# A post-norm transformer layer with a codebook FFN: GpSimd's gathers written out, ScalarE's copies moved, the 64-row first tile packed

## What is computed

```python
# x: (2, 1024, 1024); 32 heads of 32
x = layernorm(x + attention(x, wq, wk, wv, wo))          # causal, rotary
Wg = codebook[idx_gate].reshape(2752, 1024)              # codebook: (16384, 8)
Wu = codebook[idx_up].reshape(2752, 1024)
Wd = codebook[idx_down].reshape(1024, 2752)
g = x @ Wg.T;  u = x @ Wu.T
y = (silu(g) * u) @ Wd.T
x = layernorm(x + y)
```

## Time and profile before

| | |
|---|---|
| median of 3 runs | 6821.02 us (6820.23 to 6821.85) |
| the profiled execution, own time | 6826.36 us |
| its span in the trace | 6824.5 us |
| TensorE busy | 98% of the span |
| VectorE, ScalarE, GpSimd busy | 68%, 55%, 72% |
| granted TensorE clock, mean | 0.996 |

### The profile page before, as it was taken

The page is one execution under the profiler, slowest core; times in us unless marked ns, Lnnn a source line. Parts: engine busy times, 40 slices in busy tenths (PEclk is TensorE's granted clock), DMA queues, the critical chain, the costliest instruction groups (busy, mean ns, idle before and its releaser), DMA issues.

```text
span 6824.5 us, 120862 instructions
## 1 busy us (share of the span) xinstructions
PE 6664.1 (98%) x29648; PEld 4072.6 (60%) x29648; DVE 4664.4 (68%) x11403; ACT 3779.4 (55%) x6691; POOL 4936.2 (72%) x5188
## 2 busy tenths in 40 slices
PE   9999899999999999999999999999999999999998
PEld 3444565666666566666666666666666666666664
DVE  3320788887777667777677776777667776677765
ACT  0000787886666555555555555555555555556553
POOL 7777777777777777777777777777777777777771
PEclk9999999999999999999999999999999999999999
DMA  4232222233333333333333333333333333233331
GB/s 138 65 87 49 53 59 54 53 84 72 82 80 76 66 72 66 74 73 73 74 70 72 75 73 71 68 74 73 74 68 73 75 72 74 66 74 72 74 68 64
DMA packets 480031, 491.50 MB, mean 72 GB/s; under 512 B 228672, under 2 KB 349248, under 8 KB 472896
## 3 DMA queue, kind: packets, MB, share of 16 engines
q10 hardware_dynamic: 298720, 425.47, 22.3%
q0 software_dynamic: 165888, 21.57, 7.8%
q1 hardware_dynamic: 14688, 36.48, 1.4%
HBM read 426.34 MB, written 56.72 MB: 71 GB/s over the span
## 4 chain that ended last, share of the span: by engine, by line
PE 75%; ACT 1%; issue 1%; DVE 0%; ACTq 0%; DMA 0%; DVEq 0%
PE ps L420 41%; PE ps L450 18%; PE ps L468 9%; PE ps L395 3%; PE ps L431 3%; PE ps L437 1%; ACT onehot L757 0%; ACT onehot L761 0%; PE ps L406 0%; PE ps L543 0%; DVE small L1045 0%; DVE onehot L996 0%; ACT arena L852 0%; DMA arena<-code_low 0%; DVE small L1048 0%
## 5 line engine op out<-in xcount | busy, mean ns | idle before, releaser
L209 POOL DMA_INDIRECT raw<-in_codebook_dram,idx_sb x5184 | 4936.0, 952 | 1758.1 <-DMA raw<-in_codebook_dram,idx_sb 1556.3
L996 DVE TENSOR_SCALAR_CACHE_REDUCE onehot<-arena,small 128x512 fp32r<-128x512 f32 x3845 | 2622.9, 742 | 1095.7 <-PE ps L420 1054.2
L420 PE MATMUL ps<-onehot,table 128*128 128x512 f32 x12288 | 3259.1, 416 | 28.2 <-ACT onehot L761 18.5
L420 PEld LDWEIGHTS ps<-onehot,table 128*128 128x128 f32 x12288 | 2289.5, 188 | 908.8 <-issue 380.5
L757 ACT ACTIVATE onehot<-arena,small 128x512 fp32r<-128x512 f32 x2307 | 1496.6, 713 | 1170.2 <-PE ps L420 1045.2
L761 ACT ACTIVATE onehot<-onehot,small 128x512 fp32r<-128x512 f32 x2307 | 1487.3, 708 | 0.0
L450 PE MATMUL ps<-big,arena 128*128 128x512 f32 (+1 forms) x2816 | 1297.0, 597 | 0.0
L450 PEld LDWEIGHTS ps<-big,arena 128*128 128x128 f32 (+1 forms) x2816 | 514.2, 187 | 595.0 <-issue 569.6
L1003 DVE SCALAR_TENSOR_TENSOR picked<-arena,small,ps 128x512 f32<-128x512 f16 x768 | 572.0, 745 | 161.9 <-PE ps L431 146.5
L468 PE MATMUL ps<-arena 128*128 128x512 f32 (+1 forms) x1408 | 652.7, 599 | 1.8 <-ACT arena L733 1.2
L908 DVE TENSOR_REDUCE small<-ps 128x1 f32<-128x384 f32 (+7 forms) x512 | 373.9, 751 | 297.8 <-PE ps L314 294.9
(11 more groups left out here) (72 smaller groups left out, 2719.5 us busy)
## 6 DMA issues: line engine op xcount, KB each, us to landing
arena<-code_low ACTq DMA_DIRECT2D x770, 256.0 KB
arena<-code_high ACTq DMA_DIRECT2D x770, 128.0 KB
raw<-in_codebook_dram,idx_sb POOLq DMA_INDIRECT x5184
gathered_units<-raw SPq DMA_DIRECT2D x39, 512.0 KB, 3.3
arena<-gathered_units ACTq DMA_DIRECT2D x19, 1024.0 KB
queries_keys<-arena ACTq DMA_DIRECT2D x16, 1024.0 KB, 4.0
arena<-queries_keys ACTq DMA_DIRECT2D x32, 512.0 KB
big<-queries_keys ACTq DMA_DIRECT2D x32, 512.0 KB
```

The source lines that it names most:

```text
L209: pool.indirect_dma_start(raw[:, s, n, :], None, codebook, bass.IndirectOffsetOnAxis(ap=idx_sb[:, s, n:n + 1], axis=0), engine_sem=describ ...
L420: last = mm(ps[:, 4 + s % 2, :], table[:, k, c, :], onehot[:, k, :], start=(k == 0 and c == 0), stop=(k == KLO - 1 and c == PIECES - 1))
L996: dve.tensor_scalar(onehot[:, k, :], lo_sb[:, s % 2, :], kp_sb[:, k:k + 1], None, ALU.is_equal, ALU.add, accum_out=hits[:, k:k + 1]).then_ ...
```

## The change

It has three parts. The two loops of GpSimd become straight-line code with constant waits. ScalarE's order in an attention round becomes e0, e1, copies 0 to 3, e2, e3, copies 4 and 5. In step 0, the 64 gate rows and the 64 up rows are laid side by side as one 128-column weight, so that one matmul makes both (gate in PSUM rows 0 to 63, up in rows 64 to 127): 32 matmuls instead of 64. SiLU writes its result to rows 64 to 127; VectorE multiplies twice, so that `hT` holds the same 64 rows twice, and `d_rep` is filled twice as well. The 32 down matmuls of step 0 then use rows 0 to 63 and 64 to 127 in turn. A slot of step 0 holds two FFN matmuls instead of three.

```diff
-                with pool.Fori(p0, p1) as p:
+                for p in range(p0, p1):
                     for s in range(2):
                         gather_unit(c, s, P, 16 * p + 16, 16 * p, 2 * P * p + (s * P - P + CS * CS))
...
-                one = mm(ps[0:ni, 2 * (t % 2) + m, :], w_rep[:, m, k, 0:ni], big1[:, k, t * N:(t + 1) * N],
+                one = mm(ps[:, 2 * (t % 2) + m, :], w_rep[:, m, k, :], big1[:, k, t * N:(t + 1) * N],
...
-                        pe.wait_ge(d_ready, 1 + step // NTILE)
+                        pe.wait_ge(d_ready, 2 + step // NTILE)
...
-                mm(ps[:, d % banks, :], d_rep[0:ni, h * P:(h + 1) * P], hT[0:ni, t * N:(t + 1) * N],
+                rows = half_rows(h % 2) if isinstance(step, int) and step == 0 else slice(0, P)
+                mm(ps[:, d % banks, :], d_rep[rows, h * P:(h + 1) * P], hT[rows, t * N:(t + 1) * N],
                    start=True, stop=True).then_inc(down_done, 1)
...
+                if isinstance(step, int):
+                    if n < CS * NT:
+                        gate_up(step, n // CS, 0, n % CS)
+                    else:
+                        down(step, n - CS * NT)
...
-                    for n in range(3 * s, 3 * s + 3):
-                        ffn_matmul(step, ni, n)
+                    beside = 2 if isinstance(step, int) else 3
+                    for n in range(beside * s, beside * s + beside):
+                        ffn_matmul(step, n)
...
                 if turned:
-                    copy_turned(i, u - 1, 0)
-                    copy_turned(i, u - 1, 1)
+                    for j in range(4):
+                        copy_turned(i, u - 1, j)
                 if scored:
                     exponent(i, u, 2)
-                if turned:
-                    copy_turned(i, u - 1, 2)
-                    copy_turned(i, u - 1, 3)
-                if scored:
                     exponent(i, u, 3)
...
-            def turned(count, ni, bank):
+            def turned(count, rows, bank):
                 act.wait_ge(turn_done, count)
-                act.copy(d_rep[0:ni, :].rearrange("p (h c) -> p h c", h=2),
-                         ps[0:ni, bank:bank + 2, :]).then_inc(d_ready, 1)
+                for out_rows in rows:
+                    act.copy(d_rep[out_rows, :].rearrange("p (h c) -> p h c", h=2),
+                             ps[0:out_rows.stop - out_rows.start, bank:bank + 2, :]).then_inc(d_ready, 1)
...
+                gates = (4, 8, 12, 16) if isinstance(step, int) and step == 0 else (2, 7, 13, 18)
...
-                                act.wait_ge(up_done, NT)
                                 act.wait_ge(taken, 3)
...
+                if isinstance(step, int) and step == 0:
+                    rows = half_rows(1)
+                    dve.tensor_tensor(hT[half_rows(0), cols], hT[rows, cols], ps[rows, 2 * (t % 2), :],
+                                      ALU.mult).then_inc(short_ready, 1)
+                    dve.wait_ge(short_ready, t + 1)
+                    dve.tensor_tensor(hT[rows, cols], hT[rows, cols], ps[rows, 2 * (t % 2), :],
+                                      ALU.mult).then_inc(hT_ready, 1)
+                else:
+                    dve.wait_ge(up_done, step * NT + (t + 1 - NT))
```

## The result

| | before | changed |
|---|---|---|
| median | 6821.14 us (5 runs, 6820.23 to 6822.56) | 6752.44 us (5 runs, 6748.72 to 6756.50) |
| ratio | | 0.9899, interval 0.9885 to 0.9913 |
| span of the profiled execution | 6824.5 us | 6750.5 us |
| step 0 | 222.6 us | 178.4 us |
| first to last of the 128 attention rounds | 869.2 us | 842.9 us |

The account below looks back on a forecast made before the run. TensorE's own work, three quarters of the span, bounds the kernel. Step 0's 44 plus the attention's 18 less 0.5 made 61.5 us, cut to 59.5 by GpSimd: 6821.0 - 59.5 = 6761.5 us, range 6753 to 6790.

Parts of the forecast that it names:

- the cap in the sum: At slot 20 of step 19, GpSimd's unit 38 cuts TensorE's gain from 61.5 to 59.5 us.
- GpSimd's room: Lead of unit 38 at slot 20 of step 19: 29.6 + 29 = 58.6 us, plus about 1 from ScalarE.
- The attention: ScalarE's new order saves TensorE's wait for copy 2 in rounds (1, 6): net 18 us less, bounds 5 and 24.
- The delay of 0.17: Attention rounds (0, 7) end later, delaying the next (1, 6) round: 0.17 us, taken off 0.75, times 32.
- Step 0, slots 0 to 15: Gate and up slots go from 6.57 to 5.36 us, plus 1 from later SiLU: 20.4 us less.
- Slots 16 to 31: Step 0's down slots go at VectorE's pace, 5.46 us each: 85.4 us against 110.3, 24 less.
- Step 0 together: Both halves of step 0: 20.4 + 24 = 44 us less, 34 if the matmul pairs don't overlap.
- The gathers don't get faster: Rival: the loop-turn gaps come back in straight-line code, holding TensorE at slot 20 of step 19; 6790 us, 1 in 10.
- slower: straight-line code is fetched too slowly: Rival: over 10,000 GpSimd instructions in a row slow each gather; at 0.02 us more, 6892 us; 3 in 100.
- The row halves don't overlap: Rival: step 0's down matmuls on different row halves run in turn; gain 51.5, time 6769 us, 1 in 10.
- ScalarE's order gives next to nothing: Rival: the new attention order gives only 5 us; gain 49 or less, time 6772 to 6778, 2 in 10.
- More than forecast: Rival: GpSimd's other pauses shrink too; gain 61.5, or up to 67 with 24 in the attention; 6754 to 6759, 1 in 10.

Follow-up runs that it names:

- e1_gathers_only: The kernel before with GpSimd's loops written out and nothing else: 6821.7 us, ratio 0.9998.
- e2_loops_kept: The changed kernel with GpSimd's two loops put back: 6785.3 us, ratio 0.9942 to the kernel before.
- e3: The kernel before with ScalarE's new order in the attention and nothing else: 6798.2 us, ratio 0.9963.
- e4: The kernel before with the packed step 0 only, GpSimd's loops and ScalarE's old order kept: 6786.0 us, ratio 0.9948.
- e7: The changed kernel with all 32 down matmuls of step 0 on rows 0 to 63: 6768.6 us, ratio 0.9918 to the kernel before.
- e8: The kernel before with the gathers written out and one more, unused semaphore declared: 6822.8 us in one run.
- e10_short_adds: The changed kernel with every second add of step 0 on 128 of its 512 columns: 6748.9 us in one run.
- e12: The changed kernel with gate loaded in slot 20, up in slot 26, and SiLU one slot later in steps 1 to 20: 6732.8 us, ratio 0.9872.

## Why the prediction was wrong

**The step that failed** is the cap in the sum, "44 + 18 - 0.5 = 61.5 for TensorE, cut to 59.5 by GpSimd", in both of its terms. The mechanisms were right; two sizes were too small.

- *GpSimd's room.* I had "29.6 + 29 = 58.6, and ScalarE can take about 1 more". The 29.6 stands. Of the second term the loops' turns gave their 29 (`e1_gathers_only`: 28 us earlier at unit 38, alone). But in the profiled execution unit 38 was 44.4 us earlier. Of the other 15, 9 are the plain gathers, whose pace I took as fixed (the 4870 of them up to unit 38 took 6115.1 us instead of 6124.0), and 6 are the pauses of one each 128 gathers (131.0 us over the pace instead of 136.8). Both vary from one execution to the next. The "about 1" that ScalarE can take was 2.6 us in the change (held for 4.0, 1.4 lost), and 0.5 in `e2_loops_kept` (held for 36.2, 35.7 lost), where the low clock behind the wait ate most of the slack; I had no term for that. Which side of the range the time falls on was thus partly luck. In the five held executions (the changed kernel, `e2`, `e3`, `e4`, `e7`) the span ends 424.5 to 426.7 us behind the store of unit 38, whatever TensorE gained before. With unit 38 sent at 6341, as in `e1`, `e7` and `e8`, the changed kernel would by that take about 6768 us, my estimate, well inside the range. With unit 38 at 6324 it let nearly all of TensorE's gain through.
- *The attention.* I took 18 us, from 32 x (0.75 - 0.17); it gave 26.3 in the change and 25 alone. The wait at j=4 went as forecast (0.69 us in each round (1, 6), 6.93 to 6.24 on average). The delay of 0.17 did not come. Exponential 2 of a (0, 7) round did start 0.8 us later, but exponential 3 only 0.2, and the copies 4 and 5 ended 0.2 later. Before, ScalarE had stood idle for 0.19 us between them and the next first exponential; that took up the delay, and the exponential started at the same 1.36 us after the scores. The value was close to my upper bound, 24: 32 x 0.69 = 22, and 3 from the rounds (0, 7), 0.10 each, and 1 from the first round. What the subtraction missed is the idle time of 0.19 us. Without these 8 us the faster gathers would have let through 2 us more at most.

**Step 0, slots 0 to 15.** Forecast 20.4 less, measured 18.3 here and 17.9 to 19.3 in the other kernels with a packed step 0 (93.0 to 94.4 us against 112.3). A slot took 5.39. Two slots that I hadn't counted took longer: slot 4 (6.93, 0.3 over a slot with a fold) and slot 5 (5.93). And the first slot, with 8.67 us instead of 8.97, gave 0.3 instead of 1.2; it varies from 7.7 to 9.1 in the others.

**Slots 16 to 31.** Forecast 85.4, measured 84.4. The size was right and the reason half wrong, so the agreement within 1 us is partly luck. I priced the overlap at 0.9 to 1.1 us from the attention's scores, and it is 1.05; without it `e7_same_half` gives 96.6, and I had 96. But I named VectorE as what sets the pace, at 5.46 a slot. It adds two results in 1.29 us, not 1.47, when both are there at once, and its slot is 5.19 from start to start. TensorE's own average, folds included, is 83.3 / 16 = 5.21 in `e10_short_adds`, which shows that VectorE costs 1.1 us in all. The Trainium skill's rule that tiling doesn't speed up the evacuation of PSUM (TensorEngine Tiling (Array Packing), PSUM Bottleneck) is right on the direction, since VectorE went from 88.54 of 110.3 us to 80.80 of 84.4, and it decides 1 us here. The Trainium skill's rule that different tiles work in parallel (same page, Key Properties) holds for 64-row tiles of float32: 1.05 us on different halves against 1.91 on one.

**Step 0 together:** 44 forecast, 44.2 measured.

**The rivals.** "The gathers don't get faster" and "slower: straight-line code is fetched too slowly" fell with `e1_gathers_only`; the price given for the first, 6790, was 6785 in `e2_loops_kept`. The second was priced too high: unit 38 is whole after 64 + 38 x 128 = 4928 gathers, not 5056, and the 29 us of the turns were left out, so that the gain would be gone at x = 0.012 and not at 0.006, and x = 0.02 would give some 6860. "The row halves don't overlap" fell with the slots of 4.93. "ScalarE's order gives next to nothing" fell with `e3_order_only`. "More than forecast" came true: I gave it 1 in 10 and a low end of 6754, and its two ingredients were the ones named, 24 us in the attention and GpSimd's other pauses, with the gathers' pace as a third that it didn't name. The range, down to 6753, ended 0.6 us above the result.

**What came where.** To step 1 TensorE was 70.8 us ahead (26.3 in the attention, 44.2 in step 0); it lost 1.4 in step 19 and 1.6 behind it, and was 6 faster in steps 1 to 18, all of it in the slots where its own loop turns. That gives the 74.0 us between the two profiled spans. Most of the 6 belong to the profiled execution of the kernel before (3851.6 us in these steps; 3847.6 to 3848.6 in `e1`, `e3`, `e4` and `e8`), which took 5.3 us longer than the median of its runs; the medians differ by 68.7.

## What to carry to other kernels

Where an engine that runs beside the critical one feeds it late in the program, its lead is a budget: read it at each handover, by the distance from the landing of the data to the waiting instruction, and cap every gain by the smallest. Look at the next one too: with unit 38 out of the way, the last unit held TensorE for 21 us. The smallest distance was 29.6 us here, and it decided the worth of two changes that had nothing to do with GpSimd. Give such a budget the spread of the feeding engine over several executions, not one trace's value: 2 ns of 1250 in each of 5000 gathers are 10 us, as much as the forecast was off. Count a wait of TensorE dearer than its length: 3.3 us of waiting cost 6.5, and 4.9 cost 7.4. And ask of a wait for two things whether both are needed at once: loading them apart, and taking SiLU one slot after its matmul and not in the same slot, gave 22 us more than the change, 17 of them by the later SiLU with the up load in slot 26.

## What the runs showed of the hardware

- GpSimd's indirect gathers have a pace that differs between executions, in one case of the same kernel on the same chip: 1.2485 or 1.2505 us a gather, with median lengths of 944 or 947 ns.
- A turn of a GpSimd loop of 256 gathers costs 1.5 to 2.8 us, 17 turns 29 us; straight-line code of over 10,000 instructions has nothing of it (0.5 us at the same places) and runs at the pace of the loop's inside. The Trainium skill (Runtime: NRT & Kernel Launch, Instruction fetch mechanics) has a taken branch stall for the fetch, and the trace agrees with it as far as the gaps at the turns go; that a fetch fills them no row shows.
- Two float32 matmuls of K=64 on different row halves take 1.05 us together and 1.91 in turn, each with 512 columns. Against whole tiles (6.22 us) a slot with three matmuls in 64-column tiles beside the 128-row ones costs 0.35 us more (6.57), and with three in 64-row tiles 0.4 more (6.64).
- Behind a wait of 3.3 to 33 us TensorE ran at a granted clock of 0.50 for 3.4 to 6.2 us before it was back at 1.00; with that, waits of 3.29, 4.14, 4.89 and 33.05 us cost 6.5, 6.6, 7.4 and 35.7 (`e4`, `e12`, `e7`, `e2`).
